# A fused attention and feed-forward layer on one core: constants in four loads, q and k written part by part, a new order on all engines

## The chip, the cores and the metric

The kernel runs on 1 core of a Trainium2 chip. The metric is the device time of one launch in microseconds (us), lower is better. Before the change the median of 3 runs is 598.14 us (597.06 to 602.43). A difference under about 1% can't be told from no change here.

## The reference

A batch of 8 sequences of 512 tokens and 256 channels goes through a normalisation, causal attention of 16 heads of 16 channels with rotary positions, and beside it a gated feed-forward net with integer weights; their product is added to the input.

```python
x = L0_attn_x                                  # (8, 512, 256)
xn = _layernorm(x, axis=-1)
# s: attention
q = rope((xn @ wq + bq).reshape(B, S, 16, 16)); k = rope((xn @ wk + bk)...); v = (xn @ wv + bv)...
scores = einsum('bhqd,bhkd->bhqk', q, k) / 4 + causal
out = einsum('bhqk,bhkd->bhqd', softmax(scores), v)
s = out @ wo + bo
# g: feed-forward, hidden size 768, int weights scaled by 1/127
h = silu(xn @ w_gate.T) * (xn @ w_up.T)
g = silu(h @ w_down.T)
return x + s * g
```

## The kernel before, in words

One batch (one sequence) is one round of work. Five instruction queues run side by side: TensorE (PE), ScalarE (ACT), VectorE (DVE), GpSimd (POOL) and SyncE (SP), which issues nearly all DMAs. Nothing schedules them at run time: each has a list of steps, written out by hand as text tables, and a step waits on semaphores for what it needs. `START` holds the steps ahead of the repeated pattern, `SCHEDULE` one round of the pattern, `END` what is left of the last batch. A `>` behind a step means that it belongs to the next batch, `>>` to the one after that, so that in a round the attention of one batch stands beside the projections of the next. `plan` (L219) picks the table; before, START covers round 0, SCHEDULE rounds 1 to 6 and END round 7.

The steps that matter here, with their lines:

- `ST`, `RS`, `NM`: statistics of the input (DVE, L743 and L746), reciprocal root (POOL, L856 and L858), normalised input (DVE for the first batch, POOL later, L381). `XT`: its transposes on PE (L486), rounded by ACT (L653), remainder by DVE (L751).
- `W3`, `WO`, `WC`, `WT`, `SQ`: preparing the weights, once. `WC` (ACT, L642) turns the integer feed-forward weights into floats, `WT` transposes them on PE (L516) and splits them into two parts (L656, L772), `SQ` (L649) squares them for a flag that tells whether the low parts are needed.
- `QT:0` to `QT:3`: q and k of channels 0 to 127, then q and k of the rest: PE (L470), ACT writes a copy with bias (`raw`, L664), DVE the product with the cosines (`t_cos`, L759). `SW` (SP, L422 and L423) sends `raw` to `swapped` with its halves exchanged, `RO` (POOL, L868 and L871) adds the product with the sines.
- The rotated q or k is kept as three bf16 parts, each the rounding of what the one before left: `HI` (ACT, L669), `LO1` (POOL, the rest, L876), `MID` (ACT, L673), `LO2` (POOL, L881), which raise `hi_ready`, `rest_ready`, `mid_ready` and `lo_ready`.
- `WR` (SP, L430): three DMAs write the parts to `stacks` in device memory, in an arrangement of six rows per channel (`RUNS`: for k, the first part three times, the second twice, the third once; for q, the first part once beside the others, the first two, all three). `WR` waits for `lo_ready` alone. `RD:0` to `RD:3` (SP, L440) read the stacks back, q and k of four heads (a group) each.
- `A` (PE L543, DVE L783): scores with queries on the partitions, whose row maxima DVE takes; 40 steps per batch, ten per group. `MX` (DVE, L791 to L799) splits the negated maxima in three, `T2` transposes them (PE L532, ACT L678), `MP` (SP, L443) sends them into rows of `q_st`. `B` (PE L556, ACT L685): the scores again, with the maxima subtracted inside the matmul, and their exponentials; 40 steps. `SM` (POOL, L888) masks, `PV` (PE L569) multiplies with the values, `ON`, `AT`, `OP` finish the attention.
- `G`, `U`, `HL`, `DN`: the feed-forward net. `AD`, `RES`, `OUT`: product added to the input, loaded and stored.

PE writes into seven rotating PSUM banks (`Bank`, L228), so it is at most seven steps ahead of the slower of ACT and DVE. ACT, DVE and POOL take their steps strictly in the order of their tables.

At the start, `WQ` on SP (L394) issues the loads of the first input in four pieces, then all constants in one load of 832 KB (identity, a mask of 512 columns of which only the last 128 are not zero, cosines, sines), then biases, four loads of a pattern for `k_st`, and two bias rows; `WF` the three feed-forward weights. PE's transposes of the input need the identity and wait for `const_in`; so does DVE at the very start, which copies the identity to bf16 (L723) ahead of the statistics.

Of the kernel before, what the change touches and what calls it, by code (L numbers as in the profile page):

```python
# [71 lines left out]
def col_of(c, hh, col):  # L72
# [26 lines left out]
        V:1> A:31 A:32 PV:3 B:18 U:0> V:2> T2:2 B:19 A:33 A:34 G:1> A:35 U:1> ON:0 A:36 V:3> PV:4 PV:5 A:37 A:38
        PV:6 PV:7 B:20 B:21 B:22 A:39 B:23 G:2> ON:1 QT:2> U:2> B:24 T2:3 PV:8 B:25 B:26 A:0> A:1> A:2> A:3>  # L100
        AT:0 G:3> B:27 QT:3> U:3> A:4> B:28 B:29 A:5> B:30 PV:9 PV:10 B:31 B:32 A:6> B:33 A:7> G:4> B:34 A:8>
        B:35 PV:11 B:36 A:9> B:37 B:38 A:10> G:5> U:4> B:39 A:11> U:5> T2:0> ON:2 PV:12 PV:13 PV:14 A:12> PV:15
        B:0> B:1> A:13> B:2> ON:3 A:14> A:15> B:3> DN:0> A:16> A:17> AT:1 A:18> DN:1> B:4> B:5> B:6> A:19> B:7>
# [833 lines left out]
```

## Time and profile before

| | us |
|---|---|
| median of 3 runs | 598.14 |
| the profiled execution, its own time | 597.88 |
| its span, first to last instruction | 595.9 |
| PE busy | 533.8 (90%) |
| DVE busy | 486.6 (82%) |
| ACT busy | 352.8 (59%) |
| POOL busy | 307.7 (52%) |
| DMA, mean | 132 GB/s |

The profile comes from one execution. Its busy times are shares of the span; matmuls are pipelined and their ends modelled, so the same bare work can show more or less busy time. A line like `L543 PE MATMUL ps_w<-k_st,q_st ... [1.30 <-DMA k_st<-stacks]` says that PE sat idle for 1.30 us before it and that a DMA's landing ended that. PEclk is TensorE's granted clock as a share of full speed; its two levels are 1.2 GHz (0.50) and 2.4 GHz (1.00). "SPq" is time that SP takes to issue a DMA or to take a wait.

### The profile page before, as it was taken

The page shows a single profiled execution, that of the slowest core. Times are in us where ns is not written, and L with a number is a line of the kernel's source. Part 1 is how long each engine was busy: PE and PEld are TensorE (multiplying, and loading weights), DVE is VectorE, ACT ScalarE, POOL GpSimd, SP SyncE. Part 2 cuts the span into 40 slices and gives each one's busy share as a digit, 9 for nine tenths or more (in the row PEclk, how much of TensorE's full clock was granted, in tenths as well). Part 3 has the DMA queues.
Part 4 walks back from the last instruction along what each step waited for, and adds up shares of the span by engine and source line. Part 5 has one row for each costly group of instructions (what it writes and reads, how often), then busy time and mean ns, then how long its engine had stood idle before and what let it go on. Part 6 is the DMA issues. An engine that isn't in the chain of part 4 may idle for free.

```text
span 595.9 us, 11660 instructions
## 1 busy us (share of the span) xinstructions
PE 533.8 (90%) x3849; PEld 355.1 (60%) x3849; DVE 486.6 (82%) x1594; ACT 352.8 (59%) x655; POOL 307.7 (52%) x321
## 2 busy tenths in 40 slices
PE   2598789999999999998998999899998899898884
PEld 1476465657665677557764676558664576457433
DVE  1547966899987999799795999799897999698933
ACT  1384635684467646774576746765576647674570
POOL 1273415375565657555465666555566457551430
PEclk7699998999999999999998999999999999999997
DMA  9436350615246442855154541845155442835110
GB/s 267 148 113 179 110 163 20 215 40 164 78 142 202 142 110 54 255 146 160 37 164 129 177 116 38 267 146 163 41 175 164 134 109 66 243 110 156 47 40 35
DMA packets 56701, 78.39 MB, mean 132 GB/s; under 512 B 4752, under 2 KB 45968, under 8 KB 56640
## 3 DMA queue, kind: packets, MB, share of 16 engines
q1 hardware_dynamic: 55552, 76.57, 43.7%
q10 hardware_dynamic: 1088, 1.05, 0.5%
q8 instruction: 34, 0.56, 0.4%
...
## 4 chain that ended last, share of the span: by engine, by line
PE 40%; DVE 21%; DMA 20%; SPq 5%; issue 5%; ACT 5%; POOL 3%; DVEq 0%; POOLq 0%; ACTq 0%
PE ps_w L470 20%; DMA k_st<-stacks 9%; DVE ps_w L783 9%; DMA stacks<-rot_parts 6%; PE ps_w L543 6%; PE ps_o L569 6%; PE ps_w L556 5%; SPq L430 3%; DVE h_lo L834 2%; POOL rot_parts L881 2%; DVE row_max L783 2%; DMA q_st<-mx_t 2%; DMA cst<-shape_constants 2%; DVE hid L830 2%; DVE hid L825 1%
## 5 line engine op out<-in xcount | busy, mean ns | idle before, releaser
L783 DVE CUSTOM_DVE_ANT_0 ps_w<-ps_w,cst 128x384 f32<-128x384 f32 (+3 forms) x512 | 238.3, 515 | 34.7 <-PE ps_w L543 34.2
L685 ACT ACTIVATE probs<-ps_w 128x512 f32<-128x512 f32 x320 | 175.9, 599 | 58.2 <-PE ps_w L556 53.8
L888 POOL TENSOR_SCALAR_AFFINE_SELECT probs<-probs 128x512 f32<-128x512 f32 x128 | 84.8, 677 | 139.9 <-ACT probs L685 139.8
L543 PE MATMUL ps_w<-k_st,q_st 96*128 96x384 bf16 (+3 forms) x512 | 109.4, 305 | 15.9 <-DMA k_st<-stacks 13.5
L556 PE MATMUL ps_w<-q_st,k_st 108*128 108x384 bf16 (+3 forms) x512 | 107.8, 304 | 7.3 <-DMA q_st<-mx_t 5.3
L569 PE MATMUL ps_o<-probs,vals 128*32 128x512 f32 (+3 forms) x1024 | 85.8, 448 | 1.2 <-ACT o_t L688 0.8
L470 PE MATMUL ps_w<-xt_hi,wgu_hi 128*128 128x512 f32 x192 | 84.6, 441 | 1.9 <-DVE row_max L783 0.9
L543 PEld LDWEIGHTS ps_w<-k_st,q_st 96*128 96x128 bf16 x512 | 41.2, 99 | 69.3 <-issue 25.1
L470 PE MATMUL ps_w<-xt_lo,wgu_hi 128*128 128x512 f32 x192 | 76.7, 400 | 0.0
L783 DVE DVE_READ_ACCUMULATOR2_ANT row_max<- 128x1 f32 x512 | 71.7, 140 | 0.0
L556 PEld LDWEIGHTS ps_w<-q_st,k_st 108*128 108x128 bf16 x512 | 39.8, 98 | 46.9 <-issue 14.1
L868 POOL TENSOR_TENSOR swapped<-swapped,cst 128x512 f32<-128x512 f32 x32 | 41.5, 1298 | 35.1 <-DMA swapped<-raw 34.7
L881 POOL TENSOR_TENSOR rot_parts<-swapped,rot_parts 128x512 bf16<-128x512 f32 x32 | 40.4, 1265 | 31.6 <-ACT rot_parts L673 31.6
L876 POOL TENSOR_TENSOR swapped<-t_cos,rot_parts 128x512 f32<-128x512 f32 x32 | 38.7, 1210 | 21.3 <-ACT rot_parts L669 21.2
L470 PE MATMUL ps_w<-wd_hi,h_hi 128*128 128x256 f32 x192 | 48.4, 292 | 0.0
L569 PEld LDWEIGHTS ps_o<-probs,vals 128*32 128x32 f32 x1024 | 27.2, 110 | 33.5 <-issue 27.0
L700 ACT ACTIVATE hid<-ps_w 128x512 f32<-128x512 f32 x48 | 28.8, 600 | 30.7 <-PE ps_w L470 19.9
L470 PE MATMUL ps_w<-wd_hi,h_lo 128*128 128x256 f32 x192 | 46.6, 283 | 0.0
L470 PEld LDWEIGHTS ps_w<-xt_hi,wgu_hi 128*128 128x128 f32 x192 | 36.2, 189 | 13.4 <-DVE row_max L783 3.5
L871 POOL TENSOR_TENSOR t_cos<-t_cos,swapped 128x512 f32<-128x512 f32 x32 | 41.0, 1282 | 4.6
L834 DVE TENSOR_TENSOR h_lo<-hid,h_hi 128x512 fp32r<-128x512 f32 x48 | 42.1, 890 | 0.1
L470 PEld LDWEIGHTS ps_w<-xt_lo,wgu_hi 128*128 128x128 f32 x192 | 36.1, 188 | 8.5 <-issue 0.9
...
## 6 DMA issues: line engine op xcount, KB each, us to landing
stacks<-rot_parts SPq DMA_DIRECT2D x32, 384.0 KB, 3.0
q_st<-stacks SPq DMA_DIRECT2D x32, 384.0 KB, 4.3
k_st<-stacks SPq DMA_DIRECT2D x32, 384.0 KB, 5.5
swapped<-raw SPq DMA_DIRECT2D x64, 128.0 KB, 2.3
...
stacks<-rot_parts SPq DMA_DIRECT2D x32, 128.0 KB, 3.1
...
```

The source lines that it names most:

```text
L470: last = pe.matmul(dst, w, m, start=(i == 0), stop=(i == len(terms) - 1))
L543: last = pe.matmul(dst[:, col:col + w], q_st[0:ROWS, head, q], k_st[0:ROWS, head, 0:w], start=True, stop=True)
L556: last = pe.matmul(dst[:, col:col + w], k_st[0:ROWS + MAX_ROWS, head, k], q_st[0:ROWS + MAX_ROWS, head, kt * P:SEQ], start=True, stop=True)
L569: last = pe.matmul(ps_o[32 * hh:32 * hh + 32, kt * P:SEQ], vals[:, b % 2, kt, head * VW:head * VW + 32], probs[:, slot, col:col + SEQ - kt ...
L685: nc.scalar.activation(probs[:, slot, :], w_of(item)[:, :], ACT.Exp, scale=QSCALE).then_inc(exp_done, 1)
L783: last = nc.vector.tensor_tensor_reduce(out=w_of(item)[:, col:col + w], in0=w_of(item)[:, col:col + w], in1=cst[:, C_MASK + SEQ - w:C_MASK ...
L834: nc.vector.tensor_tensor(h_lo[:, i, :], hid[:, i % 2, :], h_hi[:, i, :].bitcast(F32), ALU.subtract)\
L868: nc.gpsimd.tensor_tensor(swapped[:, i % 2, :], swapped[:, i % 2, :], cst[:, C_SIN:C_SIN + SEQ], ALU.mult).then_inc(sin_done, 1)
L871: nc.gpsimd.tensor_tensor(t_cos[:, i % 2, :], t_cos[:, i % 2, :], swapped[:, i % 2, :], ALU.add).then_inc(rot_ready, 1)
L876: nc.gpsimd.tensor_tensor(swapped[:, i % 2, :], t_cos[:, i % 2, :], rot_parts[:, i % 2, 0, :], ALU.subtract).then_inc(rest_ready, 1)
L881: nc.gpsimd.tensor_tensor(rot_parts[:, i % 2, 2, :], swapped[:, i % 2, :], rot_parts[:, i % 2, 1, :], ALU.subtract).then_inc(lo_ready, 1)
L888: nc.gpsimd.affine_select(out=v, in_=v, compare_op=ALU.is_ge, fill=0.0, base=0, pattern=[[0, 4], [1, P]], channel_multiplier=-1).then_inc( ...
```

## The change

Five things are changed.

1. The constants are cut in four and the mask loses its 384 columns of zeros in the load: identity (64 KB), cosines and sines (512 KB), later the triangle (64 KB), each with a semaphore of its own; the zeros are set by POOL. The four loads of the pattern for `k_st` become one.
2. DVE copies the identity to bf16 in the step `SQ` instead of at its very start.
3. `WR` waits for each part by itself: each of its three DMAs is issued once the part that it needs last is rounded. For k the 384 KB with the first part go first and the 128 KB with the last part last; for q it is the other way round, 128 KB first and 384 KB last.
4. `FIRST, LAST` become 0 and 8: the pattern starts a round earlier, its boundary lies elsewhere in the batch, and END is empty.
5. Every table is new.

```diff
-    mask = np.zeros((P, SEQ), np.float32)
-    mask[:, SEQ - P:] = np.where(np.arange(P)[None, :] > np.arange(P)[:, None], NEG, 0.0)
-    return np.concatenate([np.eye(P, dtype=np.float32), mask, by_row(cos, cos), by_row(-sin, sin)], axis=1).astype(np.float32)
+    triangle = np.where(np.arange(P)[None, :] > np.arange(P)[:, None], NEG, 0.0)
+    return np.concatenate([np.eye(P), triangle, by_row(cos, cos), by_row(-sin, sin)], axis=1).astype(np.float32)
...
-FIRST, LAST = 1, 6
+FIRST, LAST = 0, 8
...
-                    sp.dma_start(cst[:], consts).then_inc(const_in, 16)
-                    sp.dma_start(bias_qk[:], qk_bias).then_inc(bias_in, 16)
-                    for g in range(GROUPS):
-                        sp.dma_start(k_st[ROWS:ROWS + MAX_ROWS, 4 * g:4 * g + 4, :].rearrange("r h t -> r (h t)").bitcast(F32), max_rows).then_inc(ones_set, 16)
+                    sp.dma_start(ident, consts[:, 0:P]).then_inc(ident_in, 16)
+                    sp.dma_start(cst[:, C_COS:], consts[:, 2 * P:]).then_inc(rope_in, 16)
+                    sp.dma_start(bias_qk[:], qk_bias).then_inc(qk_bias_in, 16)
                     for dst, v in ((bias_v[:], bv), (bo_row[:], bo)):
                         sp.dma_start(dst, v.rearrange("(a d) -> a d", a=1).broadcast_to([P, DM])).then_inc(bias_in, 16)
+                    sp.dma_start(cst[:, C_COS - P:C_COS], consts[:, P:2 * P]).then_inc(triangle_in, 16)
+                    sp.dma_start(k_st[ROWS:ROWS + MAX_ROWS, :, :].rearrange("r (g h) t -> r g (h t)", g=GROUPS).bitcast(F32),
+                                 max_rows.rearrange("r (g c) -> r g c", g=1).broadcast_to([MAX_ROWS, GROUPS, 2 * SEQ])).then_inc(ones_set, 16)
...
                     chunk, which = divmod(i, 2)
-                    sp.wait_ge(lo_ready, b * 4 + i + 1)
-                    for at, n_parts, k_part in RUNS:
+                    for (at, n_parts, k_part), split in zip(RUNS if which else RUNS[::-1], (hi_ready, mid_ready, lo_ready)):
+                        sp.wait_ge(split, b * 4 + i + 1)
                         rows = stacks[b % 2, which, chunk, at:at + n_parts].rearrange("a p t -> p a t")
...
-                        pe.wait_ge(const_in, 16)
+                        pe.wait_ge(ident_in, 16)
...
-                    dve.wait_ge(const_in, 16)
-                    nc.vector.tensor_copy(ident_b[:], ident).then_inc(set_once, 1)
...
                 elif kind == "SQ":
+                    dve.wait_ge(ident_in, 16)
+                    nc.vector.tensor_copy(ident_b[:], ident).then_inc(set_once, 1)
...
+                        if n == 0:
+                            dve.wait_ge(triangle_in, 16)
+                            dve.wait_ge(mask_set, 1)
...
+                    nc.gpsimd.memset(cst[:, C_MASK:C_COS - P], 0.0).then_inc(mask_set, 1)
```

Of the tables, one line of SP's repeated pattern, before and after:

```diff
-        MP:3 RD:1> SW:3> RES:0 XN:0>> WR:2> MP:0> WR:3> RD:2> RD:3> MP:1> SW:0>> SW:1>> MP:2> WR:0>> WR:1>>
+        MP:3 XN:0>> SW:3> WR:2> RES:0 MP:0> WR:3> RD:2> RD:3> MP:1> SW:0>> OUT:0 SW:1>> WR:0>> MP:2> WR:1>>
```

Where the new order matters to the prediction, three places are shown as rows of the programs. The first is SP in the repeated pattern, from the maxima of group 2 (`q_st<-mx_t`) to the reading of the next batch's first stacks; `stacks<-rot_parts` is WR, `result<-res` OUT, `swapped<-raw` SW. Before:

```order
L443 DMA q_st<-mx_t 12x4x512 [waits mxt_ready]
L430 DMA stacks<-rot_parts 128x3x512 [waits lo_ready]
L430 DMA stacks<-rot_parts 128x2x512
L430 DMA stacks<-rot_parts 128x512
L430 DMA stacks<-rot_parts 128x3x512 [waits lo_ready]
L430 DMA stacks<-rot_parts 128x2x512
L430 DMA stacks<-rot_parts 128x512
L416 DMA result<-res 128x4x256 [waits res_ready]
L422 DMA swapped<-raw 64x512 [waits lo_ready,rest_ready,raw_ready]
L423 DMA swapped<-raw 64x512
L440 DMA q_st<-stacks 96x2048 [waits exp_done,stacks_out1,stacks_out0]
L440 DMA k_st<-stacks 96x2048
```

And after:

```order
L411 DMA stacks<-rot_parts 128x512 [waits hi_ready]
L411 DMA stacks<-rot_parts 128x2x512 [waits mid_ready]
L411 DMA stacks<-rot_parts 128x3x512 [waits lo_ready]
L424 DMA q_st<-mx_t 12x4x512 [waits mxt_ready]
L411 DMA stacks<-rot_parts 128x3x512 [waits hi_ready]
L411 DMA stacks<-rot_parts 128x2x512 [waits mid_ready]
L411 DMA stacks<-rot_parts 128x512 [waits lo_ready]
L403 DMA swapped<-raw 64x512 [waits lo_ready,rest_ready,raw_ready]
L404 DMA swapped<-raw 64x512
L421 DMA q_st<-stacks 96x2048 [waits exp_done,stacks_out1,stacks_out0]
L421 DMA k_st<-stacks 96x2048
```

WR of q stands ahead of the maxima instead of behind them, the store of the result has moved further up, and behind the last wait for `lo_ready` of k only one DMA of WR is left.

The second is ACT at the same place, from the second `raw` of a batch (k of the first channels) to the second part of that k. Before:

```order
L664 ACTIVATE raw<-ps_w,bias_qk 128x512
L688 COPY o_t<-ps_o 128x512
L669 CAST rot_parts<-t_cos 128x512
L685 ACTIVATE probs<-ps_w 128x512 x2
L700 ACTIVATE hid<-ps_w 128x512 x2
L673 CAST rot_parts<-swapped 128x512
L669 CAST rot_parts<-t_cos 128x512
L704 CAST h_hi<-hid 128x512
L678 CAST mx_t<-ps_w 12x512
L685 ACTIVATE probs<-ps_w 128x512
L673 CAST rot_parts<-swapped 128x512
```

After:

```order
L645 ACTIVATE raw<-ps_w,bias_qk 128x512
L666 ACTIVATE probs<-ps_w 128x512 x2
L681 ACTIVATE hid<-ps_w 128x512
L650 CAST rot_parts<-t_cos 128x512
L669 COPY o_t<-ps_o 128x512
L654 CAST rot_parts<-swapped 128x512
L666 ACTIVATE probs<-ps_w 128x512
L685 CAST h_hi<-hid 128x512
L666 ACTIVATE probs<-ps_w 128x512
L659 CAST mx_t<-ps_w 12x512
L650 CAST rot_parts<-t_cos 128x512
L666 ACTIVATE probs<-ps_w 128x512 x3
L654 CAST rot_parts<-swapped 128x512
```

The second HI (the second `rot_parts<-t_cos`) has moved behind the copy of the maxima `mx_t`, and the second MID behind two more exponentials.

The third is SP in the first round, between the reading of group 2's stacks and the next batch's first swap. Before:

```order
L440 DMA q_st<-stacks 96x2048 [waits stacks_out1,stacks_out0]
L440 DMA k_st<-stacks 96x2048
L410 DMA xn<-L_attn_x 128x4x256 [waits xt_ready]
L440 DMA q_st<-stacks 96x2048 [waits stacks_out1,stacks_out0]
L440 DMA k_st<-stacks 96x2048
L443 DMA q_st<-mx_t 12x4x512 [waits mxt_ready]
```

After:

```order
L421 DMA q_st<-stacks 96x2048 [waits stacks_out1,stacks_out0]
L421 DMA k_st<-stacks 96x2048
L403 DMA swapped<-raw 64x512 [waits lo_ready,rest_ready,raw_ready]
L404 DMA swapped<-raw 64x512
L424 DMA q_st<-mx_t 12x4x512 [waits mxt_ready]
L421 DMA q_st<-stacks 96x2048 [waits stacks_out1,stacks_out0]
L421 DMA k_st<-stacks 96x2048
```

The maxima of group 1 now go ahead of group 3's stacks, and the load of the third input has left this place.

## Rows read from the trace of the kernel before

**Rows 1.** The page, section 1: busy time and share of each engine.

```profile
PE 533.8 (90%) x3849; PEld 355.1 (60%) x3849; DVE 486.6 (82%) x1594; ACT 352.8 (59%) x655; POOL 307.7 (52%) x321
```

**Rows 2.** Windows: stretch, length, busy PE, PEld, DVE, ACT, POOL (instructions), PEclk, DMA share, GB/s.

```profile
18.00:75.10 57.10, 45.52 (x227) 33.58 (x226) 39.70 (x112) 35.70 (x65) 28.40 (x26) 0.90 0.42 124
75.10:149.90 74.80, 71.13 (x505) 46.41 (x504) 61.51 (x208) 42.56 (x81) 34.95 (x36) 0.95 0.40 119
...
417.00:483.80 66.80, 62.71 (x474) 42.09 (x474) 60.09 (x198) 41.91 (x80) 38.97 (x40) 1.00 0.47 138
483.80:595.90 112.10, 94.86 (x750) 59.94 (x748) 83.38 (x278) 63.65 (x120) 45.07 (x51) 0.97 0.32 93
```

**Rows 3.** Timeline of the start: start, length, engine, line, operation [idle before <-releaser].

```profile
0.79 1.82 SPq L396 DMA_DIRECT2D xn<-L_attn_x  x4
...
11.95 1.40 DVE L743 BATCH_NORM_STATS2 stats<-xn 128x6 f32<-128x256 f32 x4
...
16.88 1.94 PE L486 MATMUL ps_w<-cst,xn 128*128 128x128 f32 x8 [11.73 <-DVE xn L381]
...
23.59 0.69 ACT L664 ACTIVATE raw<-ps_w,bias_qk 128x512 f32<-128x512 f32 x1 [3.48 <-PE ps_w L470]
```

**Rows 4.** DMA issues: transfer, queue, count, KB each, median us from issue to landing.

```profile
stacks<-rot_parts SPq DMA_DIRECT2D x32, 384.0 KB, 3.0
...
stacks<-rot_parts SPq DMA_DIRECT2D x32, 128.0 KB, 3.1
...
probs<-L_ffn_w_gate SPq DMA_DIRECT2D x1, 768.0 KB, 9.4
...
xn<-L_attn_x SPq DMA_DIRECT2D x4, 128.0 KB, 3.7
```

**Rows 5.** ACT's groups, 18 to 45 us: operation, count, busy us, mean ns, idle before.

```profile
L649 ACT ACTIVATE h_lo<-probs 128x768 fp32r<-128x768 f32 x6 | 5.1, 849 | 0.1
L642 ACT CAST probs<-probs 128x1536 f32<-128x1536 int32 x3 | 4.4, 1468 | 0.0
L656 ACT CAST wgu_hi<-ps_w 128x512 fp32r<-128x512 f32 (+1 forms) x8 | 3.4, 481 | 0.0
```

**Rows 6.** Timeline, first batch: DVE's wait for the constants, last rounding, first stacks read.

```profile
11.80 0.23 DVE L723 CAST ident_b<-cst 128x128 bf16<-128x128 f32 x1 [10.55 <-DMA cst<-shape_constants]
...
39.75 1.17 POOL L881 TENSOR_TENSOR rot_parts<-swapped,rot_parts 128x512 bf16<-128x512 f32 x1 [1.14 <-ACT rot_parts L673]
...
46.20 0.33 SPq L440 DMA_DIRECT2D q_st<-stacks  x1
```

**Rows 7.** Timeline and window around PE's longest wait in the second round.

```profile
81.91 0.84 SPq L443 DMA_DIRECT2D q_st<-mx_t  x1
...
87.47 0.61 PE L556 MATMUL ps_w<-q_st,k_st 108*128 108x512 bf16 x1 [2.61 <-DMA q_st<-mx_t]
...
87.00:93.80 6.80, 6.33 (x26) 3.05 (x27) 3.05 (x13) 1.78 (x4) 2.55 (x2) 0.50 0.07 16
```

**Rows 8.** Timeline of a repeated round: second HI on ACT, second LO2 on POOL.

```profile
368.82 0.62 ACT L669 CAST rot_parts<-t_cos 128x512 bf16<-128x512 f32 x1 [0.85 <-POOL t_cos L871]
...
372.36 1.16 POOL L881 TENSOR_TENSOR rot_parts<-swapped,rot_parts 128x512 bf16<-128x512 f32 x1 [0.73 <-ACT rot_parts L673]
```

**Rows 9.** The chain that ended last, 370 to 386 us: start, us, what.

```profile
370.73 0.86 SPq L443
...
374.92 1.07 SPq L430
...
379.56 5.85 DMA k_st<-stacks
```

**Rows 10.** Waits from 149.9 to 483.8 us (total, times, longest); a window as in rows 2.

```profile
DVE ps_w L783 <- PE ps_w L543: 20.3, 9, 4.7
...
PE ps_w L543 <- DMA k_st<-stacks: 8.7, 6, 2.2
...
319.10:322.50 3.40, 3.40 (x18) 0.73 (x18) 2.19 (x4) 0.60 (x2) 1.76 (x2) 0.50 0.38 100
```

More of the change, by code:

```diff
@@ L99 @@
[L99 to L103, printed above, removed]
@@ new lines @@
+        T2:0 HL:3 MID:3 G:4 G:5 B:0 HL:4 B:1 B:2 HL:5 B:3 B:4 XT:0> XT:1> B:5 DN:0 DN:1 B:6 QT:0> B:7 T2:1 B:8
+        B:9 B:10 B:11 B:12 QT:1> B:13 HI:0> B:14 B:15 G:0> B:16 B:17 PV:3 MID:0> G:1> HI:1> T2:2 B:18 MID:1>
+        B:19 B:20 B:21 HL:0> B:22 PV:7 B:23 B:24 HL:1> QT:2> B:25 T2:3 G:2> B:26 B:27 G:3> AT:0 HL:2> HI:2>
+        HL:3> QT:3> B:28 B:29 B:30 G:4> B:31 B:32 B:33 MID:2> G:5> HL:4> B:34 PV:11 B:35 B:36 HI:3> B:37 T2:0>
+        B:38 B:39 MID:3> PV:15 HL:5> B:0> B:1> B:2> B:3> AT:1 DN:0> B:4> DN:1> B:5> B:6>
@@ L139 @@
+        A:28 QT:1> A:29 A:30 V:1> MX:2 V:2> G:0> A:31 G:1> A:32 ON:0 A:33 A:34 V:3> A:35 U:0> A:36 A:37 U:1>
+        A:38 A:39 HL:0> MX:3 QT:2> ON:1 HL:1> G:2> A:0> U:2> A:1> G:3> AT:0 U:3> A:2> HL:2> A:3> QT:3> HL:3>
+        G:4> A:4> U:4> A:5> A:6> A:7> G:5> A:8> NM:0> A:9> MX:0> HL:4> A:10> A:11> U:5> NM:1> ON:2 A:12> NM:2>
+        A:13>
     """,
     "pool": """
-        WQ RS:0 WO:0 RO:0 RO:1 LO1:0 RS:0> LO1:1 LO2:0 LO2:1 NM:0> NM:1> RO:2 RO:3 LO1:2 NM:2> NM:3> LO1:3 LO2:2
-        LO2:3 SM:0 SM:1 SM:2 RO:0> LO1:0> SM:3 RO:1> LO2:0> SM:4 LO1:1> LO2:1> SM:5 SM:6 RO:2> SM:7 LO1:2> SM:8
@@ L143 @@
-        RO:3> LO1:3> SM:9 SM:10 LO2:2> SM:11 LO2:3> RS:0>> NM:0>> NM:1>> NM:2>> NM:3>> AD:0 SM:0> SM:1> AD:1
-        SM:2> RO:0>> LO1:0>> SM:3> RO:1>> LO2:0>> LO1:1>> SM:4> LO2:1>> SM:5> SM:6> SM:7> RO:2>> SM:8> LO1:2>>
-        SM:9> RO:3>> LO2:2>> LO1:3>> SM:10> SM:11> LO2:3>> SM:0>>
+        WQ RS:0 WO:0 RO:0 LO1:0 RO:1 LO2:0 LO1:1 LO2:1 RO:2 RS:0> NM:0> NM:1> LO1:2 LO2:2 RO:3 NM:2> LO1:3 LO2:3
+        NM:3> SM:0 SM:1 SM:2 RO:0> LO1:0> RO:1> SM:3 LO1:1> LO2:0> SM:4 LO2:1> SM:5 SM:6 RO:2> SM:7 SM:8
@@ L169 @@
[L169 removed]
+        XT:0>> B:7> XT:1>> T2:1> B:8> QT:0>> B:9> B:10> G:0>> B:11> QT:1>> B:12> B:13> G:1>> HI:0>> PV:3>
+        MID:0>> B:14> HL:0>> B:15> T2:2> HI:1>> B:16> B:17> B:18> MID:1>> B:19> G:2>> QT:2>> B:20> HL:1>> B:21>
+        B:22> PV:7> B:23> B:24> B:25> T2:3> B:26> B:27> AT:0> HI:2>> B:28> QT:3>> B:29> G:3>> HL:2>> MID:2>>
+        HL:3>> B:30> B:31> PV:11> B:32> G:4>> B:33> B:34> HL:4>> B:35> B:36> HI:3>> G:5>> B:37> T2:0>> B:38>
@@ L178 @@
+        A:4>> A:5>> A:6>> A:7>> A:8>> G:4>> A:9>> NM:0>> U:4>> HL:3>> MX:0>> A:10>> HL:4>> G:5>> U:5>> NM:1>>
+        A:11>> ON:2> A:12>> NM:2>> A:13>>
     """,
     "pool": """
-        RS:0>> NM:0>> NM:1>> NM:2>> NM:3>> SM:1> AD:0 AD:1 SM:2> RO:0>> LO1:0>> RO:1>> SM:3> LO2:0>> LO1:1>>
-        LO2:1>> SM:4> SM:5> SM:6> RO:2>> SM:7> SM:8> LO1:2>> LO2:2>> SM:9> RO:3>> SM:10> LO1:3>> SM:11> LO2:3>>
-        SM:0>>
+        LO1:2> RO:3> LO2:2> SM:9 LO1:3> SM:10 SM:11 LO2:3> RS:0>> NM:0>> NM:1>> SM:0> NM:2>> NM:3>> AD:0 SM:1>
@@ L183 @@
+        SM:2> AD:1 RO:0>> SM:3> LO1:0>> RO:1>> LO2:0>> LO1:1>> LO2:1>> SM:4> SM:5> RO:2>> SM:6> SM:7> SM:8>
     """,
     "sp": """
-        MP:3 RD:1> SW:3> RES:0 XN:0>> WR:2> MP:0> WR:3> RD:2> RD:3> MP:1> SW:0>> SW:1>> MP:2> WR:0>> WR:1>>
-        OUT:0 SW:2>> RD:0>>
+        MP:3 XN:0>> SW:3> WR:2> RES:0 MP:0> WR:3> RD:2> RD:3> MP:1> SW:0>> OUT:0 SW:1>> WR:0>> MP:2> WR:1>>
+        SW:2>> RD:0>> RD:1>>
     """,
 }
-FIRST, LAST = 1, 6
+FIRST, LAST = 0, 8
 END = {
     "pe": """
-        PV:12 ON:2 PV:13 PV:14 PV:15 ON:3 AT:1 OP:0 OP:1
```

105 lines of the change are left out of this document (38 added, 67 removed).

## The prediction, on record before the changed kernel was run

> **What bounds the kernel now.** I read the page first. PE is busy for 533.8 of the span's 595.9 us and DVE for 486.6 [rows 1], so some 60 us at most can come out of waiting. Next the windows by batch [rows 2], which show four stages. Up to XT:0 of the first batch it is 18.0 us. The first round takes 57.1 us, with PE busy 45.5. The second takes 74.8, the longest. From there to 483.8 come five rounds of (483.8 - 149.9) / 5 = 66.8 us each, of which the last shows PE busy for 62.7 and DVE for 60.1; then 112.1 us for the last batch. So PE and DVE together hold the repeated rounds, 4 and 7 us short of full, while the start and the second round are far from full.
>
> The start shows why: DVE sits idle 10.55 us in front of its copy of the identity, until the 832 KB of constants land [rows 6], although the statistics behind it need only the input, whose pieces are issued from 0.79 to 2.6 us [rows 3] and take 3.7 us to land [rows 4]. PE's first transpose comes at 16.88 us [rows 3].
>
> In a repeated round the chain of waits [rows 9] leaves the engines at 370.7 us and runs through SP's queue: the maxima, six DMAs of WR until 376.0, the store, the swap, then 5.85 us in which the stacks are read. The list of waits [rows 10] gives its price over the five rounds: DVE waits 20.3 us for A's matmuls, PE 8.7 us for the stacks. The longest of these PE waits, 2.2 us, has a second price: behind it the granted clock is 0.50 for 3.4 us (319.1 to 322.5), which takes 1.7 us of PE's work.
>
> **The start.** The last piece of the input should land at about 2.2 + 3.7 = 5.9 us. The four statistics then end some 0.4 us later, at 6.3 instead of 11.95 + 1.40 = 13.35, and all up to PE's first transpose moves with them: about 10 us instead of 16.88. The identity (64 KB, directly behind the input in the queue) should be there by 6.4, if it takes what a 128 KB piece of the input does. For the zeros and the bf16 copy I charge nothing: POOL sets the zeros while it waits for DVE's statistics, and the copy (0.23 us, rows 6) falls into DVE's idle stretches at the weights; without that cover it would cost its 0.23 us.
>
> Not all of the 6.9 us arrives. ACT now takes the first weight conversion (WC:0) ahead of the first `raw`, and that waits for weights issued at about 6.5 us that take 9.4 to land [rows 4]: 15.9. Then 1.47 for WC:0 [rows 5] and some 0.6 for WO put the first `raw` at 18.0, against 23.59 [rows 3]: 5.6 us earlier. From there ACT has some 16.6 us of work up to the second MID: three `raw` at 0.69, two WC at 1.47, six squares at 0.85 with what reads their sums (together 5.7), seven WT at 0.48 [rows 5], four roundings at 0.62 [rows 8]. So k's last rounding (LO2:1) ends at about 36 instead of 39.75 + 1.17 = 40.9 [rows 6]: 4.9 us earlier.
>
> Then the new WR counts. Before, RD:0 is issued at 46.20, 5.3 us behind the end of LO2:1 [rows 6]. After, one issue counts, and it lands 3.1 us after its start [rows 4]: with SP's own steps some 3.6. Gain 1.7, so the first scores come 6.6 us earlier. Behind them, DVE has HL:0, HL:1, G:2 and QT:3 of the first batch done already, in time in which it waited before: four instructions of about 0.7 us, of which I count half, 1.4. The start is worth **8 us** (4.5, if the feed-forward weights land no earlier than ACT gets to them now and ACT becomes the bound, to 11).
>
> The two sizes of WR land after 3.0 (384 KB) and 3.1 us (128 KB) [rows 4]: size does not matter, only the issues ahead do. The Trainium skill (DMA: Bandwidth & Descriptors, "Anatomy of one DMA") puts a DMA at some 2.0 us plus its bytes at 436 GB/s, fitted on another issue path than this one; by that the 128 KB would land 0.6 us sooner than 384 KB, and by that estimate the sum below would be 7 x 0.6 = 4 us larger. The sum goes by the rows.
>
> **The second round.** Its 74.8 us are 8 more than a repeated round. PE waits 2.61 us for the maxima of group 1, issued at 81.91 right behind a large read and landed 5.5 us later; the clock is then at 0.50 for 6.8 us, of which PE works 6.33 [rows 7]. That is 2.6 + 3.2 = 5.8 us. After the change the maxima go ahead of group 3's read (the third place in the order). Other waits remain in this round, so I count **4 us**, between 0 and 8 (its whole excess over a repeated round).
>
> **A repeated round.** On SP the chain loses the maxima and the six issues; what is late next is the rounding itself. Before, LO2:1 ended at 373.5 [rows 8], WR was issued until 376.0, the store and the swap until 378.9, RD:0 at 379.0, and the stacks were there at 385.4 [rows 9]. After, the second HI stands behind `mx_t`, which SP saw ready at 370.7, so it begins 1.9 us later than its 368.8 [rows 8]. LO1 takes 1.2 us beside three exponentials of 0.6, MID then ends at 373.7 and LO2:1 at 375.0. The last DMA of WR starts there and lands at 378.1, the swap fits in between, and RD:0 follows at 378.1, 0.9 us earlier than before. So of 4.4 us of issue time that WR had, less than 1 us is left as a gain; the order of ACT gives the rest back.
>
> More comes from what stands ahead of the first scores. On DVE, MX:2 (four small instructions, about 1 us) and AT:0 (0.7) have come in front of A:0 and G:0 (0.7) has gone; on PE, QT:3 (about 1.45) has come and G:3 (1.0) has gone. So DVE waits about 0.9 + 1.0 = 1.9 us less of its 20.3 / 5 = 4.1, and PE has up to 0.9 + 0.45 = 1.35 us to set against its 8.7 / 5 = 1.7: its wait nearly goes, and with it the fall of the clock. Late next are PE itself and the maxima of group 0, which have 3.6 us of PE work between T2:0 and B:0 and need some 4.5 (issue, 0.86 [rows 9], and about 3 to land); before it was much the same.
>
> If all PE waits for the stacks went and the clock held, a round would gain 1.7 + 1.7 / 5 = 2.0 us or a little more; if the new order makes a wait of its own instead, it may lose 0.5. I take 1.35, the PE term alone, over six waits (batches 2 to 7; that of batch 1 is in the second round): **8 us**, from -3 to +14. In the last 112.1 us the same pieces run out; there I count 0, within 2 us either way.
>
> **The sum.** 8 + 4 + 8 = 20 us off the profiled execution's own 597.88 give 577.9. That execution lies 0.26 us under the median of 598.14, so: **578.0 us**.
>
> **The rivals.**
>
> (a) Only the start is gained. For it: in rounds of 66.8 us PE and DVE are busy for 63 and 60 [rows 2], seven banks couple them, and k's second part is rounded later than before. A new order then costs in small waits what it saves at A:0. Against it: the wait is one place, with 20.3 us of DVE and 8.7 of PE [rows 10]. Time: 597.9 - 8 = 590, or 593 at the low end of the start.
>
> (b) Slower, by the late rounding. HI behind `mx_t` means behind PE's whole row of steps up to T2:2, and any slip of MX:2 on DVE now delays k of the next batch as well. If k's last part is 3 us later than I worked out, RD:0 is issued at 381 and the first scores come 2 us later than before. PE then waits 3.7 instead of 1.7 us, and behind each such wait loses 1.7 us to the clock [rows 10]: 3.7 us per round, times 6 = 22, less 8 for the start and 4 for the second round: 604, and 608 if the second round keeps its wait. It ends slower than before from a slip of about 2 us upward. Against it: ACT is busy for 41.9 us of a round of 66.8 [rows 2], so most steps put in front of HI move into idle time.
>
> (c) More than forecast: nearly all of the waits and of the second round's excess go, 9 + 7 + 14 = 30: 568.
>
> The Trainium skill (DMA: Bandwidth & Descriptors, "Queues, rings and completion order") says that a DMA's semaphore rises only after every earlier write of the same DMA engines; that speaks against small loads in a busy queue, since the identity would count as landed no sooner than the input ahead of it. By that rule the sum is the same, because PE needs both; the 5.5 us that 48 KB of maxima take behind large reads [rows 7] agree with it.
>
> **How the numbers follow.** The forecast (570 to 587) gets 0.62, (a) 0.20, (b) 0.08, (c) 0.10. A measurement of this kernel tells 1%, 6 us, from no change. (a) lies around that bound: half of it, 0.10, is faster by over 1%, half within. Faster: 0.62 + 0.10 + 0.10 = 0.82; within 1%: 0.10; slower: 0.08. The range leaves out (b) and the far end of (c): 565 to 594.
>
> **What would show it.** Right: PE's first transpose at about 10 us, the first `raw` near 18, RD:0 of the first batch near 39.6, no wait of 2 us for `q_st<-mx_t` in the second round and no half clock there; rounds of about 65.4 us between XT:0 of batches 2 and 7, with about 11 instead of 20.3 us of DVE's waits for A's matmuls in them; the last batch again 112. Wrong in part: a first `raw` as late as 21 (then the feed-forward weights hold the start), or rounds of 66.8 with the wait only moved. Wrong altogether: rounds above 69 us with PE waiting for `k_st<-stacks` and a clock of 0.50 behind it, which is (b).

## The result, and the profile after

The changed kernel takes 561.15 us (median of 4, 560.90 to 566.29) beside 598.36 us for the kernel before: ratio 0.9388, 95% interval 0.9318 to 0.9458. The prediction said 578.0 us, range 565 to 594. The sign was right; the gain is 37 us where 20 were forecast, and the time lies below the range. The profiled execution has an own time of 560.90 us and a span of 558.8.

The page, section 1 (answers to [rows 1]), and windows with the boundaries at XT:0 of each batch (answers to [rows 2], columns as there):

```profile
PE 518.8 (93%) x3849; PEld 347.5 (62%) x3849; DVE 470.7 (84%) x1594; ACT 349.0 (62%) x655; POOL 298.4 (53%) x322
```

```profile
13.70:66.50 52.80, 44.19 (x220) 32.08 (x219) 39.41 (x107) 33.63 (x62) 27.67 (x24) 0.97 0.56 168
66.50:138.40 71.90, 69.74 (x521) 46.18 (x518) 62.63 (x219) 43.82 (x83) 35.88 (x39) 1.00 0.49 138
138.40:452.00 313.60, 309.45 (x2362) 208.67 (x2361) 285.21 (x981) 206.69 (x390) 188.97 (x200) 1.00 0.52 147
452.00:558.80 106.80, 94.27 (x749) 59.37 (x748) 79.70 (x276) 63.49 (x120) 43.48 (x51) 0.97 0.34 98
```

Put beside [rows 2], the 37 us come from these places:

| stretch | before | after | gain | forecast |
|---|---|---|---|---|
| start and first round | 75.1 | 66.5 | 8.6 | 8 |
| second round | 74.8 | 71.9 | 2.9 | 4 |
| five repeated rounds | 333.9 (66.8 each) | 313.6 (62.7 each) | 20.3 | 6.75 |
| last batch | 112.1 | 106.8 | 5.3 | 1.35 |

So the terms of the start and of the second round held within about a microsecond, and the repeated round gained 4.1 us instead of 1.35. Its waits, over the five rounds (answers to [rows 10]), first of PE, then two of DVE:

```profile
PE ps_w L513 <- DVE mx_nat L783: 2.3, 3, 0.8
PE ps_w L524 <- DMA k_st<-stacks: 0.7, 2, 0.4
PE ps_w L537 <- DMA q_st<-mx_t: 0.2, 1, 0.2
...
DVE at_lo L796 <- ACT at_hi L672: 8.7, 5, 2.0
...
DVE ps_w L767 <- PE ps_w L524: 7.1, 14, 1.2
```

PE's wait for the stacks has gone from 8.7 to 0.7 us, DVE's for A's matmuls from 20.3 to 7.1. And the list is short: three lines for PE. The same view of the kernel before has seven, that of [rows 10] and six more:

```profile
PE ps_w L578 <- DVE row_max L783: 2.3, 4, 0.6
PE ps_w L532 <- DVE mx_nat L799: 2.1, 3, 1.3
PE ps_w L543 <- DVE row_max L783: 0.9, 1, 0.9
PE ps_w L556 <- DVE hid L830: 0.8, 3, 0.3
PE ps_w L556 <- DMA q_st<-mx_t: 0.8, 1, 0.8
PE ps_w L556 <- DVE row_max L783: 0.3, 1, 0.3
```

Together 15.9 us before and 3.2 after: 12.7 / 5 = 2.5 us a round. That is all that PE's idle time fell by (66.8 - 63.5 = 3.3 us a round before, 62.7 - 61.9 = 0.8 after). The prediction had counted the line of [rows 10] only.

SP's queue in the round from 326.7 (timeline, answers to [rows 9]), and POOL's steps with k's second rounding (answers to [rows 8]):

```profile
341.67 5.41 SPq L411 DMA_DIRECT2D stacks<-rot_parts  x3
347.12 0.86 SPq L424 DMA_DIRECT2D q_st<-mx_t  x1
348.03 2.04 SPq L411 DMA_DIRECT2D stacks<-rot_parts  x3
351.06 0.50 SPq L403 DMA_DIRECT2D swapped<-raw  x1
351.60 0.60 SPq L404 DMA_DIRECT2D swapped<-raw  x1
352.30 0.52 SPq L421 DMA_DIRECT2D q_st<-stacks  x1
```

```profile
344.29 1.28 POOL L856 TENSOR_TENSOR t_cos<-t_cos,swapped 128x512 f32<-128x512 f32 x1
345.53 1.16 POOL L866 TENSOR_TENSOR rot_parts<-swapped,rot_parts 128x512 bf16<-128x512 f32 x1
346.65 1.15 POOL L861 TENSOR_TENSOR swapped<-t_cos,rot_parts 128x512 f32<-128x512 f32 x1
348.54 1.17 POOL L866 TENSOR_TENSOR rot_parts<-swapped,rot_parts 128x512 bf16<-128x512 f32 x1 [0.73 <-ACT rot_parts L654]
```

```profile
345.69 0.61 ACT L650 CAST rot_parts<-t_cos 128x512 bf16<-128x512 f32 x1
```

The first row of SP is WR of q: its three DMAs lie over 5.4 us, because each waits for its own part, and the last is out before the maxima at 347.12. Counted from XT:0 of the batch (326.7 after, 350.9 before), the second `LO2` begins at 21.8 us (before 372.36 - 350.9 = 21.5) and RD:0 at 25.6 (before 379.0 - 350.9 = 28.1): 2.5 us earlier.

Of the DMA issues (answers to [rows 4]):

```profile
stacks<-rot_parts SPq DMA_DIRECT2D x32, 384.0 KB, 2.9
...
stacks<-rot_parts SPq DMA_DIRECT2D x32, 256.0 KB, 3.1
stacks<-rot_parts SPq DMA_DIRECT2D x32, 128.0 KB, 2.4
```

The start, lines picked from the timeline (answers to [rows 3] and [rows 6]):

```profile
8.58 0.43 DVE L724 BATCH_NORM_STATS2 stats<-xn 128x6 f32<-128x256 f32 x1 [0.98 <-DMA xn<-L_attn_x]
...
12.53 1.94 PE L467 MATMUL ps_w<-cst,xn 128*128 128x128 f32 x8 [12.53 <-DVE xn L360]
...
18.84 0.68 ACT L645 ACTIVATE raw<-ps_w,bias_qk 128x512 f32<-128x512 f32 x1
...
33.80 1.17 POOL L866 TENSOR_TENSOR rot_parts<-swapped,rot_parts 128x512 bf16<-128x512 f32 x1 [0.73 <-ACT rot_parts L654]
...
39.59 0.34 SPq L421 DMA_DIRECT2D q_st<-stacks  x1
```

### The profile page after: what moved, and what is told of

The parts are those of the page before. It is cut to its first block, busy times and chain, and to the rows that moved or that the text cites. A ratio compares the mean times of both kernels' runs of the same rounds, so it can differ in the third digit from the quotient of the medians.

```text
span 558.8 us, 11660 instructions
## 1 busy us (share of the span) xinstructions
PE 518.8 (93%) x3849; PEld 347.5 (62%) x3849; DVE 470.7 (84%) x1594; ACT 349.0 (62%) x655; POOL 298.4 (53%) x322
## 4 chain that ended last, share of the span: by engine, by line
PE 45%; DVE 22%; DMA 14%; ACT 7%; issue 6%; POOL 3%; SPq 1%; DVEq 0%; ACTq 0%; POOLq 0%
PE ps_w L451 24%; DVE ps_w L767 11%; PE ps_w L524 7%; PE ps_w L537 6%; PE ps_o L550 5%; DMA k_st<-stacks 5%; DMA q_st<-mx_t 4%; DMA stacks<-rot_parts 3%; DVE hid L814 2%; DVE row_max L767 2%; ACT probs L666 2%; DVE hid L809 2%; DMA probs<-L_ffn_w_gate 2%; DMA q_st<-L_attn_wv 1%; DVE t_cos L740 1%
## 5 line engine op out<-in xcount | busy, mean ns | idle before, releaser
L666 ACT ACTIVATE probs<-ps_w 128x512 f32<-128x512 f32 x320 | 178.7, 598 | 40.1 <-PE ps_w L537 38.4
L873 POOL TENSOR_SCALAR_AFFINE_SELECT probs<-probs 128x512 f32<-128x512 f32 x128 | 78.9, 635 | 76.9 <-ACT probs L666 76.5
L537 PE MATMUL ps_w<-q_st,k_st 108*128 108x384 bf16 (+3 forms) x512 | 105.8, 302 | 2.9 <-DMA q_st<-mx_t 1.8
L451 PE MATMUL ps_w<-xt_hi,wgu_hi 128*128 128x512 f32 x192 | 87.3, 455 | 0.1
L550 PEld LDWEIGHTS ps_o<-probs,vals 128*32 128x32 f32 x1024 | 25.9, 109 | 31.8 <-issue 19.6
L866 POOL TENSOR_TENSOR rot_parts<-swapped,rot_parts 128x512 bf16<-128x512 f32 x32 | 37.6, 1176 | 8.0 <-ACT rot_parts L654 8.0
L685 ACT CAST h_hi<-hid 128x512 fp32r<-128x512 f32 x48 | 29.5, 616 | 19.7 <-DVE hid L814 19.7
L809 DVE SCALAR_TENSOR_TENSOR hid<-hid,ps_w 128x512 f32<-128x512 f32 x48 | 32.7, 683 | 10.3 <-ACT hid L681 9.8
```

The source lines that it names most:

```text
L451: last = pe.matmul(dst, w, m, start=(i == 0), stop=(i == len(terms) - 1))
L537: last = pe.matmul(dst[:, col:col + w], k_st[0:ROWS + MAX_ROWS, head, k], q_st[0:ROWS + MAX_ROWS, head, kt * P:SEQ], start=True, stop=True)
L550: last = pe.matmul(ps_o[32 * hh:32 * hh + 32, kt * P:SEQ], vals[:, b % 2, kt, head * VW:head * VW + 32], probs[:, slot, col:col + SEQ - kt ...
L666: nc.scalar.activation(probs[:, slot, :], w_of(item)[:, :], ACT.Exp, scale=QSCALE).then_inc(exp_done, 1)
L809: nc.vector.scalar_tensor_tensor(out=hid[:, i % 2, :], in0=hid[:, i % 2, :], scalar=1.0, in1=w_of(item)[:, :], op0=ALU.add, op1=ALU.mult). ...
L866: nc.gpsimd.tensor_tensor(rot_parts[:, i % 2, 2, :], swapped[:, i % 2, :], rot_parts[:, i % 2, 1, :], ALU.subtract).then_inc(lo_ready, 1)
```

## The experiments

Four pieces are told apart: C, the constants in pieces with the later bf16 copy; W, the split writes; S, the one place in SyncE's repeated order (WR:0 ahead of MP:2, and the store behind SW:0); E, the new orders of the other engines with all else in the tables. Each run is compared with runs of the kernel before on the same chip: 596.56 us beside the first four, 598.96 (589.78 to 604.59, no interval given) beside the next four, 599.66 beside the four from sp_only to cw_sp, 598.09 beside eng_c and out_late. Medians are over 4 to 10 runs. A ratio is the run's time over that of the kernel before, with its 95% interval; where two runs from different chips are set against each other, the difference of their ratios is given too. Rounds, waits and clocks are those of each run's one profiled execution.

### c_only: C alone, all tables old

```diff
-                    sp.dma_start(cst[:], consts).then_inc(const_in, 16)
+                    sp.dma_start(ident, consts[:, 0:P]).then_inc(ident_in, 16)
+                    sp.dma_start(cst[:, C_COS:], consts[:, 2 * P:]).then_inc(rope_in, 16)
```

> The kernel before with parts 1 and 2 of the change alone (constants in four loads, bf16 copy in SQ); old WR, old tables. Both theories of the round expect its rounds unchanged at 66.8 us. PE's first transpose should come near 10 to 12 us instead of 16.9. If the start is held by the constants alone, the whole gain of some 5 us is carried to the end: 593. If ACT's preparation of the feed-forward weights holds it, less arrives: 596 to 598.

Measured 593.65 us, 0.9938 [0.9900, 0.9976], which is 1 to 6 us of gain. The start and first round take 71.5 us, 3.6 less than before: XT:0 comes 4.8 us earlier, and the first round gives a part back.

### w_only: W alone

```diff
-                    sp.wait_ge(lo_ready, b * 4 + i + 1)
-                    for at, n_parts, k_part in RUNS:
+                    for (at, n_parts, k_part), split in zip(RUNS if which else RUNS[::-1], (hi_ready, mid_ready, lo_ready)):
+                        sp.wait_ge(split, b * 4 + i + 1)
```

> The kernel before with part 3 alone (WR waits part by part); old constants, old tables. Theory WRITES (the repeated round was shortened because the parts are written earlier): rounds of 64 to 65 us instead of 66.8, total about 585. Theory ORDER (it was shortened by the order): SP comes to WR of q only after the maxima of group 2, when all three parts are ready, so all six issues still stand behind each other; rounds 66.3 to 66.8, total 595 to 599.

Measured 593.37 us, 0.9930 [0.9884, 0.9976]; rounds of 66.5 us. DVE's wait for A's matmuls stays at 20.2 us. With WR:0 still behind MP:2, its parts are ready when SP comes to it, and waiting for each alone brings little: 3 us by the medians, nearer to the theory ORDER (595 to 599) than to WRITES (585).

### o_only: all tables new (E and S), constants and writes as before

> The kernel before with parts 4 and 5 alone (new tables and boundary); old constants, old WR that waits for the last part. Theory WRITES: rounds of 66 us or more, total about 590. Theory ORDER: rounds of 63 to 64 us, DVE's waits for A's matmuls over five rounds under 12 us, total about 567 to 572 (the start 4 to 6 us later than in the changed kernel, and 1 us per round for WR).

Measured 578.60 us, 0.9704 [0.9655, 0.9754]. Rounds of 63.9 us and 11.3 us of DVE's waits are what ORDER said; the total lies 7 us above its 567 to 572, and 11 under the 590 of WRITES.

### oc: the changed kernel with W undone (C, E, S)

> The changed kernel with the old WR (all three DMAs behind the last part), all else changed. Theory WRITES: rounds back to 66 us or more, total 580 or more. Theory ORDER: two issues of 0.5 us each and no more come between the last rounding of k and the reading of the stacks; PE's wait for k_st<-stacks grows from 0.1 to about 1 us per round, rounds 63.5 to 64, total 566 to 569.

Measured 573.71 us, 0.9605 [0.9565, 0.9646]; rounds of 64.0 us. The rounds are again those of ORDER, the total is in neither range. So W, worth 3 to 4 us alone, is worth 12.6 us on top of the rest (13 by the ratios). The pieces don't add up one by one, and the next runs look for the pair that belongs together.

### w_sp: the kernel before with W and S

```diff
-        SW:0>> SW:1>> MP:2> WR:0>> WR:1>> OUT:0 SW:2>>
+        SW:0>> OUT:0 SW:1>> WR:0>> MP:2> WR:1>> SW:2>>
```

> The kernel before with the new WR and, in SP's repeated pattern alone, the order of the changed kernel at one place: store of the result behind the first swap, WR of q ahead of the maxima of group 2. All other tables old. Theory QUEUE (most of what the order gave per round is SP's queue: the maxima no longer stand ahead of WR): RD:0 some 2 us earlier, rounds of 64.5 to 65.5 us, total about 586. Theory ENGINES (it came from the order on PE, DVE, ACT and POOL): DVE waits 1 to 2 us less at the first scores and the rest stays, rounds 65.8 to 66.5, total 591 to 594.

Measured 576.21 us (575.05 to 576.40), 10 us below what the nearer theory gave and 22 to 23 us under the kernel before. That baseline scatters; w_mp below, which differs from w_sp by the place of the store alone, has the same rounds and a ratio with an interval (0.9641). The constants and the orders of PE, ACT, DVE and POOL are those of before. (Here and below, a diff of a table shows only the part of its line that changes.) The window over its five rounds and all of PE's waits there:

```profile
146.90:466.40 319.50, 312.61 (x2364) 210.45 (x2363) 294.43 (x983) 208.32 (x390) 196.76 (x201) 1.00 0.51 147
```

```profile
PE ps_w L577 <- DVE row_max L782: 2.3, 4, 0.6
PE ps_w L531 <- DVE mx_nat L798: 1.4, 3, 0.5
PE ps_w L469 <- DVE xt_lo L750: 1.0, 4, 0.2
PE ps_w L542 <- DVE row_max L782: 0.9, 1, 0.9
PE ps_w L555 <- DVE hid L829: 0.5, 2, 0.3
PE ps_w L555 <- DVE row_max L782: 0.3, 1, 0.3
PE ps_w L555 <- DMA q_st<-mx_t: 0.2, 1, 0.2
```

Rounds of 63.9 us, the wait for the stacks gone from PE's list (8.7 us before), the clock at 1.00 throughout: one piece of SP's order and the split writes bring 2.9 of the round's 4.1 us. The other waits have stayed: these seven lines sum to 6.6 us, the six besides the stacks in the kernel before to 7.2.

### sp_old: the changed kernel with S undone (C, E, W)

> The changed kernel with that one place of SP's repeated pattern put back (maxima of group 2 ahead of WR of q, store between WR of k and the swap). Theory QUEUE: rounds of 65 us or more. Theory ENGINES: RD:0 about 1 us later, PE's wait for k_st<-stacks grows from 0.1 to 0.5 to 1 us a round, rounds 63.2 to 63.8, total 564 to 567.

Measured 576.28 us (573.41 to 578.81), beside the same scattered baseline: 15 us over the changed kernel, where the theory that trusted the engines' orders gave 564 to 567. Rounds of 65.6 us; PE waits 10.4 us for the stacks over five of them.

### mx_early: the changed kernel with MX:3 ahead on DVE

In the changed kernel the fourth instruction of MX:3 takes 1.25 us beside a multiplication of two SBUF operands on POOL, and PE waits 0.74 us behind it (round from 326.7; the same happens in three of the five rounds, not in every one as the text below has it).

```diff
-        A:39> HL:1>> QT:2>> MX:3> V:3>>
+        A:39> MX:3> HL:1>> QT:2>> V:3>>
```

> The changed kernel with the four small instructions of MX:3 on DVE moved ahead of HL:1 and QT:2 of the next batch, in the repeated pattern. In the changed kernel the last of the four takes 1.26 us instead of 0.19 in every round, beside the first multiplication of RO:2 on POOL. Theory PORT (two-operand work of DVE and POOL on SBUF shuts each other out): all four take 0.17 to 0.19 us, PE's wait of 0.7 us for T2:3 goes, rounds 62.0 to 62.3, total 557 to 560. Theory CHAIN (the long one is only a late semaphore and PE is full anyhow): rounds 62.7 and total 561 as before.

Measured 563.62 us (561.13 to 565.71), rounds of 63.1 us: no gain. The four small instructions no longer meet POOL's: the one of L783 falls from a mean of 348 to 187 ns over the five rounds, as these rows of the groups show, first of the changed kernel, then of this one:

```profile
L783 DVE TENSOR_TENSOR mx_nat<-mx_rest,mx_nat 128x16 bf16<-128x16 f32 x20 | 7.0, 348 | 0.7
```

```profile
L783 DVE TENSOR_TENSOR mx_nat<-mx_rest,mx_nat 128x16 bf16<-128x16 f32 x21 | 3.9, 187 | 0.7
```

But PE now waits for QT:2, which stands behind them (PE's first wait of this kernel over the same rounds):

```profile
PE ps_w L537 <- DVE t_cos L740: 4.4, 5, 0.9
```

### hl_moved: the kernel before with HL:0 and HL:2 later on DVE

```diff
-        HL:0>> V:3>> NM:0> A:35> NM:1>
+        V:3>> NM:0> A:35> HL:0>> NM:1>
...
-        G:3>> HL:2>> A:1>> AT:0>
+        G:3>> A:1>> HL:2>> AT:0>
```

> The kernel before with two remainders of the feed-forward net on DVE (HL:0, HL:2) moved one or two steps back, out of the time in which POOL subtracts for q and k. Theory PORT: DVE's instructions that take longer than their like sum to 1.0 to 1.5 us a round instead of 2.4, and the part that stood behind the first scores comes off the round: 66.0 to 66.4 us, total 593 to 596. Rival: the stacks' landing sets the round, DVE only waits longer there, rounds 66.8 and total 597.

Measured 599.43 us (597.65 to 600.46): no gain. The mean of `h_lo` in the five rounds is 892 ns before, 766 here and 686 in the changed kernel:

```profile
L834 DVE TENSOR_TENSOR h_lo<-hid,h_hi 128x512 fp32r<-128x512 f32 x30 | 26.3, 892 | 0.0
```

```profile
L832 DVE TENSOR_TENSOR h_lo<-hid,h_hi 128x512 fp32r<-128x512 f32 x30 | 22.5, 766 | 0.0
```

3.8 us of DVE's busy time went, its wait for A's matmuls is 27.1 us instead of 20.3, and the kernel is no faster. That the slow `h_lo` cost the kernel before its time is thereby excluded for at least this part of it.

### sp_only, w_mp, w_out: which part of S, and whether it needs W

All three have the engines' orders and the constants of before. sp_only has S with whole writes. w_mp has W and only the first of these edits, w_out has W and only the second:

```diff
-        SW:0>> SW:1>> MP:2> WR:0>> WR:1>> OUT:0 SW:2>>
+        SW:0>> SW:1>> WR:0>> MP:2> WR:1>> OUT:0 SW:2>>
...
-        SW:0>> SW:1>> MP:2> WR:0>> WR:1>> OUT:0 SW:2>>
+        SW:0>> OUT:0 SW:1>> MP:2> WR:0>> WR:1>> SW:2>>
```

> The kernel before with only the one place in SyncE's order changed: the store of the result behind SW:0 and WR:0 ahead of MP:2, but the rotated q still written when all of it is ready. Theory ORDER (the place in the queue alone frees the round, the split writes add little): 576 to 580, rounds of 64. Theory PAIR (WR:0 can only use the place ahead of MP:2 if its first parts are written before the low part is ready; whole, it is issued 1.9 us later and the read of q comes only about 1 us earlier than before instead of 2.1): 587 to 592, rounds of 65.5 to 66.

> The kernel before with the split writes and WR:0 ahead of MP:2, the store of the result left where it was (behind WR:1). Theory MAXIMA (the maxima held up WR:0): about 577 to 580, the read of q at 27.5 us behind the first xt instead of 29.4. Theory STORE (the store of 0.7 us ahead of SW:2 held up the second half): 590 to 593, as with the split writes alone.

> The kernel before with the split writes and the store of the result moved ahead to behind SW:0, MP:2 left ahead of WR:0. Theory MAXIMA: 588 to 593, since the write of q still starts behind the maxima. Theory STORE: 577 to 582.

Measured: sp_only 586.60 us, 0.9785 [0.9721, 0.9848]; w_mp 578.14 us, 0.9641 [0.9617, 0.9665]; w_out 588.62 us, 0.9790 [0.9758, 0.9823]. PAIR holds (586.6 beside 587 to 592, and not 576 to 580), and so does MAXIMA (578.1 and 588.6). In times from XT:0 of the batch, means of four rounds, from the traces:

| | WR of q issued until | MP:2 until | RD:0 issued until | A:0 on PE begins | round |
|---|---|---|---|---|---|
| before | 22.5 | 20.6 | 29.2 | 34.4 | 66.8 |
| w_only | 22.1 | 20.4 | 29.4 | 34.6 | 66.5 |
| w_out | 22.1 | 20.5 | 29.1 | 34.0 | 65.6 |
| sp_only | 21.0 | 21.9 | 27.7 | 32.7 | 65.1 |
| w_mp | 19.8 | 20.7 | 26.9 | 32.4 | 63.9 |
| w_sp | 19.8 | 20.7 | 27.1 | 32.4 | 63.9 |

Before, SP stands at MP:2 until 20.6 us, although q is rounded at 19.4. Put ahead and whole, WR:0 needs until 21.0 and pushes the maxima back. Put ahead and split, two of its three issues are out before q's last part is ready, and the maxima pass at 20.7, as late as ever: nothing is paid for the new place. k's write then begins at once, and RD:0 comes 2.1 to 2.3 us earlier. The store is not nothing either: w_out has some 8 us on w_only (0.9790 against 0.9930, intervals apart). Once WR:0 stands ahead of the maxima, its place makes 2 us at most (w_sp against w_mp).

### cw_sp: the changed kernel without E

> All of the change but the new order on TensorE, ScalarE, VectorE and GpSimd: constants in four loads, split writes, and SyncE's order at the one place. Theory ENGINES FEW (the new engine orders bring what the table of rounds shows, 1.2 us a round and some 3 at the start and end): 570 to 574. Theory ENGINES NONE (the rest of the gap to the changed kernel is the start alone): 560 to 566.

Measured 575.08 us, 0.9595 [0.9566, 0.9623]. That is above both ranges (570 to 574, 560 to 566), nearer to the theory that E brings a few us: E is worth 575.1 - 561.2 = 13.9 us with the other pieces in place (12.4 by the ratios, 0.9595 and 0.9388). By the traces 6 of them lie in the five rounds (64.0 against 62.7), 4.1 in the start and first round (70.6 against 66.5), 2.0 in the second.

### eng_c: C and E alone, and out_late: only the store put back

```diff
-        SW:0>> OUT:0 SW:1>> WR:0>> MP:2> WR:1>> SW:2>>
+        SW:0>> SW:1>> MP:2> WR:0>> WR:1>> OUT:0 SW:2>>
...
-        SW:0>> OUT:0 SW:1>> WR:0>> MP:2> WR:1>> SW:2>>
+        SW:0>> SW:1>> WR:0>> MP:2> WR:1>> OUT:0 SW:2>>
```

The first edit is eng_c's, which has whole writes besides; the second is out_late's.

> The changed kernel with the split writes undone and SyncE's one place put back, so the constants in pieces and the new engine orders alone. Theory ON TOP (the new engine orders gain only where the read of q comes early; the write of q behind the maxima, whole, costs what it costs before): the split writes are worth 12.5 us in the new order with the queue's place, and the place 15 us with the split writes; without both the cost adds up to 20 to 27 us on the changed kernel's time, 581 to 588. Theory OWN (the engine orders have a gain of their own, and the two pieces overlap in the new order, since either loss alone already brings the wait and the half clock): 574 to 579.

> The changed kernel with only the store of the result put back behind WR:1, the maxima left behind WR:0. Theory MAXIMA (the store is beside the path, as it was on the old engine orders, where it made 2 us or nothing): 560 to 564, rounds of 62.7. Theory STORE (in the changed kernel its 0.7 us ahead of the swap of group 2 delay that group): 565 to 569, rounds of 63.5 or more.

Measured: eng_c 587.74 us, 0.9824 [0.9772, 0.9876]; ON TOP holds (581 to 588). Its profiled execution (593.36) lies 5.6 us above that median, so its rows are read for the pattern and not for the microsecond. Its start and first round take 67.6 us, 7.5 less than before, but the repeated rounds of this execution 67.9, a microsecond more than before:

```profile
140.60:480.20 339.60, 321.24 (x2363) 214.36 (x2361) 284.15 (x981) 207.29 (x390) 189.22 (x200) 0.96 0.48 136
```

```profile
PE ps_w L523 <- DMA k_st<-stacks: 17.7, 9, 3.4
```

```profile
DVE ps_w L766 <- PE ps_w L523: 31.2, 22, 4.4
```

PE waits twice as long for the stacks as before (17.7 against 8.7 us) and the granted clock is at 0.50 for 27 us of these rounds (6.8 before). So the new engine orders alone bring the repeated round no gain. That they make it longer is not shown: if the 5.6 us lie in these five rounds, the median has rounds of 67.9 - 5.6 / 5 = 66.8 us (an estimate), as before. On the whole E does gain by itself, since c_only is at 0.9938 and eng_c at 0.9824, intervals apart: some 7 us, none of it in the repeated rounds. And only one wait is left in PE's list, the one for the stacks; those for DVE, which stay in w_sp, are gone.

out_late: 566.72 us (564.35 to 568.44), 0.9467 [0.9419, 0.9515]. The expectation STORE gave 565 to 569, and the profiled rounds are 63.9 us, with 7.1 us of waits for the stacks. The intervals of this ratio and of the changed kernel's still touch (0.9419 and 0.9458), so a part of the store, up to some 5 us, is likely and not shown. On the old orders it was 2 us at most once the maxima were behind (w_mp against w_sp). No version tried beat the changed kernel.

## Why the prediction was wrong in size

**The start (said 8, was 8.6): right, and in part by luck.** PE's first transpose came at 12.5 us, not about 10: the last statistic starts at 8.58, since the input's last piece lands then and not at 5.9. But the first `raw` came at 18.84 (said 18.0) because WC:0, waiting for its weights, set it in either case. `LO2` of k ended at 35.0 (said 36), and RD:0 came 4.6 us behind it (said 3.6): two steps off by a microsecond, in opposite directions, put RD:0 at 39.59 (said 39.6). The bf16 copy of the identity, charged at nothing, took 1.00 us at 28.46 instead of 0.23, and its cover held: DVE waits 1.84 us for ACT's squares behind it. Put together differently than forecast: 3.6 us come with C alone, 7.5 with C and E, 8.6 with W and S.

**The second round (said 4, was 2.9): right within its range.** Its clock is 1.00 and the 2.61 us of PE's wait for the maxima [rows 7] are gone. eng_c, with neither W nor S, has a second round of 73.0 and the same clock: 1.8 of the 2.9 us are the new order's doing.

**The repeated round (said 1.35 of at most 2.0 "or a little more", was 4.1): the step that failed.** Three parts of it did: the time of RD:0, what the order of ACT gives back, and the cap on what a round can gain.

First, RD:0 was to come 0.9 us earlier and came 2.5 earlier. The prediction let the second HI start behind `mx_t`, 1.9 us later than before, and k's last rounding 1.5 us later. It starts 1.1 us later (19.0 against 17.9 us from XT:0). It does stand behind `mx_t`, but that comes 0.7 us earlier than before (345.21 - 326.7 against 370.13 - 350.9), and POOL's product, which it needs, ends at 345.57 in any case. The second `LO2` is only 0.4 us later: in both kernels `LO1` waits for POOL to end the first `LO2`, which has a mask less ahead of it now. The step held `mx_t` at its old time and left POOL out. The last 128 KB then land 2.4 us after their issue, not 3.1. The 3.1 of [rows 4] was of a DMA directly behind two larger ones. The estimate by the Trainium skill that the prediction set aside (DMA: Bandwidth & Descriptors, "Anatomy of one DMA", 0.6 us less for 128 than for 384 KB) comes near the 2.9 and 2.4 measured here, but not near the 256 KB, which took 3.1.

Second, what is given back. The prediction rightly took the maxima and five of the six issues out of the chain, but let the order of ACT take all of that back but 0.9 us. w_sp has the old order on ACT and the changed kernel the new one, and RD:0 is issued 25.8 and 26.0 us from XT:0 (28.3 before; means of four rounds, where 2.5 above is of one): the new order costs 0.2. And the prediction gave the new place of WR of q and the split no worth as a pair: the place costs nothing only when the write is split, as the table above shows.

Third, the cap. It took one of seven waits of PE (8.7 of 15.9 us) and half of one of two stretches of slow clock. The stacks' wait falls from 8.7 to 0.7 us, which is 1.6 us a round. The six others fall from 7.2 to 2.5, which is 0.9. They don't hang on the stacks: w_sp has no wait for the stacks and still has 6.6 us of others. They go with E: in eng_c none is left. So W and S take the one wait and E takes the others, and together 2.5 us of idle time go. Another 1.6 us are busy time of PE: 317.4 before, from the windows of the five rounds, and 309.5 after. Half of the 6.8 us at a clock of 0.50 makes 0.7 a round. The other 0.9 is not explained; w_sp, whose clock is 1.00, has 312.6, so some 0.6 of it go with E. Whether that is work done faster or time that the modelled ends of matmuls hide stays open.

**The last batch (said nothing beyond the round that runs into it, 1.35, was 5.3).** The prediction had 0 for its own pieces. It takes 108.2 us in w_sp with the old engine orders and 110.1 in eng_c with the new ones, so W and S bring 3.9 there and C and E 2.0.

**The rivals.** (a) is out, since most of the gain lies in the repeated rounds. (b), slower by the late rounding, was not the changed kernel. eng_c has its signs, waits for the stacks of 3.5 us a round and the clock falling beside them, but not its cause: k's last `LO2` starts 21.9 us from XT:0 there as in the changed kernel, and what differs is the write of q, whole and behind the maxima. The sum recorded for (b) was wrong too: 597.9 + 22 - 8 - 4 is 608 and not 604, and 612 if the second round keeps its wait. (c) had the right direction, 568, and even it was too small.
